# Thirty-two-row score products in attention, and batches taken in pairs through the layers before it

## The reference

```python
x = x + L0_xattn(_layernorm(x), ctx_1024)        # local attention-free mixing, then LN, 128->512->128 MLP, LN
x = x + L0_ffn(_layernorm(x))                    # gated FFN with 8-bit-like rounding of rows and ternary weights
x = x + L1_xattn(_layernorm(x), ctx, ctx, mask)  # 16 heads of 8 dimensions, 256 keys, softmax
x = x + L1_ffn(_layernorm(x))                    # top-1 routing to one of 8 experts, 128->256->128, gelu
```

## Time and profile before

| quantity | us |
|---|---|
| median of three runs | 248.2 |
| profiled execution | 249.16 |
| its span | 247.3 |
| PE busy | 192.6 (78%) |
| DVE busy | 173.2 (70%) |
| ACT busy | 135.4 (55%) |
| POOL busy | 119.1 (48%) |
| mean granted TensorE clock | 0.952 |

### The profile page before, as it was taken

The page is one execution under the profiler, slowest core; times in us unless marked ns, Lnnn a source line. Parts: engine busy times, 40 slices in busy tenths (PEclk is TensorE's granted clock), DMA queues, the critical chain, the costliest instruction groups (busy, mean ns, idle before and its releaser), DMA issues.

```text
span 247.3 us, 4771 instructions
## 1 busy us (share of the span) xinstructions
PE 192.6 (78%) x1750; PEld 134.4 (54%) x1750; DVE 173.2 (70%) x454; ACT 135.4 (55%) x271; POOL 119.1 (48%) x231
## 2 busy tenths in 40 slices
PE   0479865998328479776989988988897895999994
PEld 0358653897203177552433543543555784798883
DVE  4678888994684979869767786886755655739252
ACT  2246744939476578435767567667794256260100
POOL 8131768996649857831587784784221022000000
PEclk9999999999955789998899999999999997999999
DMA  5895040000000000000000000000000000000000
GB/s 169 324 398 219 0 170 4 0 4 0 3 1 0 0 0 3 3 3 3 0 0 5 1 0 3 0 3 0 3 1 3 0 0 4 0 3 21 24 21 21
DMA packets 4461, 8.75 MB, mean 35 GB/s; under 512 B 514, under 2 KB 3026, under 8 KB 4052
## 3 DMA queue, kind: packets, MB, share of 16 engines
q1 hardware_dynamic: 3636, 7.78, 8.4%
q10 hardware_dynamic: 800, 0.63, 0.8%
HBM read 7.89 MB, written 0.52 MB: 34 GB/s over the span
## 4 chain that ended last, share of the span: by engine, by line
PE 31%; POOL 29%; DVE 19%; issue 9%; ACT 7%; DMA 2%; SPq 1%; POOLq 0%; DVEq 0%
PE ps L1252 28%; POOL gate_pt L514 6%; POOL rstd L380 5%; POOL w L400 3%; PE ps L1261 3%; POOL x_in L431 3%; DMA wf<-weights_dram 2%; POOL w L392 2%; POOL vareps L377 2%; DVE gate_pt L1033 2%; DVE mx L1090 2%; DVE amax L1027 2%; DVE stats L798 2%; DVE half_c L1080 2%; ACT gate_pt L758 1%
## 5 line engine op out<-in xcount | busy, mean ns | idle before, releaser
L1090 DVE TENSOR_REDUCE mx<-ps 128x2 f32<-128x512 f32 x64 | 42.2, 686 | 16.6 <-PE ps L1252 16.5
L758 ACT ACTIVATE gate_pt<-ps 128x512 f32<-128x512 f32 x64 | 37.2, 603 | 15.6 <-PE ps L1252 15.3
L1252 PE MATMUL ps<-w,hid_xm 128*128 128x256 f16 (+1 forms) x288 | 30.3, 263 | 0.1
L514 POOL TENSOR_SCALAR gate_pt<-ka_mem 32x256 f16<-32x256 f16 x64 | 25.5, 399 | 4.4
L1252 PE MATMUL ps<-gate_pt,half_c 128*128 128x512 f16 x64 | 25.0, 393 | 3.2 <-issue 1.9
L1252 PEld LDWEIGHTS ps<-w,hid_xm 128*128 128x128 f16 x288 | 25.4, 101 | 3.4 <-issue 0.4
L1252 PE MATMUL ps<-qb,gate_pt 128*128 128x256 f16 x128 | 25.4, 281 | 0.8
L1261 PE MATMUL ps<-cst,rows 128*128 128x128 f32 x32 | 7.5, 333 | 18.0 <-ACT rows L662 8.8
L1252 PE MATMUL ps<-gate_pt,hid_xm 128*32 128x256 f32 x256 | 20.4, 390 | 1.5 <-ACT gate_pt L758 1.5
L1252 PEld LDWEIGHTS ps<-qb,gate_pt 128*128 128x128 f16 x128 | 9.5, 99 | 18.7 <-issue 11.4
L380 POOL TENSOR_TENSOR rstd<-vareps,halfs 128x2 f32<-128x2 f32 x24 | 17.7, 738 | 2.0
(11 more groups left out here) (221 smaller groups left out, 505.6 us busy)
## 6 DMA issues: line engine op xcount, KB each, us to landing
stage<-weights_dram SPq DMA_DIRECT2D x2, 1024.0 KB, 11.1
wf<-weights_dram SPq DMA_DIRECT2D x4, 256.0 KB, 8.5
wf<-mask_dram SPq DMA_DIRECT2D x1, 1024.0 KB, 4.8
eb_oT<-ffw_dram SPq DMA_DIRECT2D x1, 768.0 KB, 8.2
ctx_in<-ctx_rows_dram ACTq DMA_DIRECT2D x4, 128.0 KB, 5.9
x_in<-x_dram SPq DMA_DIRECT2D x4, 128.0 KB, 3.1
gate_pt<-ctx_cols_dram SPq DMA_DIRECT2D x1, 512.0 KB, 8.5
out_dram<-ctx_in SPq DMA_DIRECT2D x4, 128.0 KB, 1.7
```

The costliest lines, as they stand in the source:

```text
L514: ins = nc.gpsimd.tensor_scalar(kz[part, n % KRING, k], ka[part, b, quad], 1.0, 0.0, ALU.mult, ALU.add)
L758: nc_act(pt[:, head % PRING].rearrange("p t n -> p (t n)"), ps[:, 2 + head % 2, :], ACT.Exp, scale=DK ** -0.5).then_inc(sig["probs"], 1)
L1090: V.tensor_reduce(mx[:, b, head:head + 2, t], score_bank(4 * n + i).rearrange("p (h n) -> p h n", h=2), AX.X, ALU.max).then_inc(sig["smax" ...
L1252: return nc.tensor.matmul(dst, lhsT, rhs, start=start, stop=stop, skip_group_check=True)
```

## The change

Four edits come together.

1. Attention. The ring `kz`, its zeroing and `separated_keys` are gone. Score products take the 32 rows of one head directly from `ka`, `qa` and `qb`. A step issues four 256-column products (shifted tile 0, plain tile 0, shifted tile 1, plain tile 1); shifted head k lies in row strip k and the plain head in strip PLAIN_HEADS[k]. `weighted_values` goes from steps 0 and 1 of a quad to steps 0 and 2.
2. Routing of a batch on DVE is cut in three parts, at places 12, 13 and 14 of a tail; before it was one piece at place 13.
3. Pairs. Roots of LN_A (batches 2 and 3), LN_OUT and LN_FFN are taken for two batches in one instruction; the mean times root of LN_FFN goes to DVE; quantisation scales are computed for two batches at a time; the quantised rows, products and gate tiles of batches 0 and 1 are put ahead of the norms of batches 2 and 3.
4. Order. On PE the first and second MLP products of the batches are interleaved. On POOL the `beta` addition is gone (it is one DVE instruction over 128x1024 values now, ahead of DVE's split of `y`, together with the split of the key biases), the gated products come ahead of weight splits, and the splits of `wq` and `wo1` come later. On ACT the weight copies and the context copy move.

```diff
-KRING = 4
+PLAIN_HEADS = (2, 3, 0, 1)
-TAIL_STEPS = (0, 2, 4, 6, 10, 13, 15)
+TAIL_STEPS = (0, 2, 4, 6, 10, 12, 15)
+ROUTE_AT = (12, 13, 14)
...
-            def rstd_of(ln, b):
+            def rstd_of(ln, *bs):
+                cols = slice(bs[0], bs[-1] + 1)
+                pool.wait_ge(sig["ln_moments"], nth_norm(ln, bs[-1]))
...
+                nc.gpsimd.tensor_tensor(rstd[:, ln, cols, :].rearrange("p b t -> p (b t)"),
+                                        vareps[:, ln, cols, :].rearrange("p b t -> p (b t)"),
+                                        halfs[:, 0:len(bs) * TILES], ALU.pow).then_inc(sig["ln_rstd"], 1)
...
+            gated(0)
+            gated(1)
             a, z = SEG["wo"]
             pool.wait_ge(sig["w_hi"], 2)
...
+            gated(2)
+            gated(3)
             split_lo("w1", 3)
+            rstd_of(LN_A, 0)
+            rstd_of(LN_A, 1)
+            rstd_of(LN_A, 2, 3)
             split_lo("w2", 4)
...
-            for b in range(B):
-                for t in range(TILES):
-                    ins = nc.gpsimd.tensor_tensor(xb[:, b, t], x_in[:, b, t], beta_b[:, :], ALU.add)
...
             for first in range(0, B, 2):
-                for b in (first, first + 1):
-                    rstd_of(LN_OUT, b)
-                for b in (first, first + 1):
-                    rstd_of(LN_FFN, b)
-                    rows_shift(LN_FFN, b)
+                rstd_of(LN_OUT, first, first + 1)
+                rstd_of(LN_FFN, first, first + 1)
...
-            def separated_keys(n):
...
-                for k in range(4):
-                    part = slice(32 * k, 32 * k + 32)
-                    ins = nc.gpsimd.tensor_scalar(kz[part, n % KRING, k], ka[part, b, quad], 1.0, 0.0, ALU.mult, ALU.add)
...
+            ffn_rows(0)
+            ffn_rows(1)
...
+            round_rows(0)
+            round_rows(1)
+            key_hi(0, 0)
+            key_hi(1, 0)
+            quantised_columns(0)
+            quantised_columns(1)
+            gate(0)
+            gate(1)
+            ffn_rows(2)
+            ffn_rows(3)
...
+            V.tensor_tensor(xb[:, :, :, :].rearrange("p b t n -> p (b t) n"), x_in[:, :, :, :].rearrange("p b t n -> p (b t) n"),
+                            beta_b[:, :].unsqueeze(1).to_broadcast([P, B * TILES, D]), ALU.add).then_inc(sig["xb"], 1)
+            dve.wait_ge(sig["mbias_hi"], 1)
+            V.scalar_tensor_tensor(kb16[0:2, :], kb_h[:, :], c("lo_2", 2), kb_in[:, :], ALU.mult, ALU.add)\
+                .then_inc(sig["mbias_ready"], 1)
...
+            def scores_tile(n, i, t, masked):
+                b, quad = divmod(n, QUADS)
+                head = rows_of(PLAIN_HEADS[i])
+                dst = score_bank(i)[:, t * T:(t + 1) * T]
+                ins = mm(dst, qa[head, b, quad, t * P:(t + 1) * P], ka[head, b, quad], True, not masked)
...
+            def shifted_tile(n, k, t, masked):
+                b, quad = divmod(n, QUADS)
+                tok = slice(t * P, (t + 1) * P)
+                dst = ps[:, 2 + k % 2, t * T:(t + 1) * T]
+                ins = mm(dst, ka[rows_of(k), b, quad, tok], qb[rows_of(k), n % 2], True, not masked)
...
+            def shifted_beside_plain(n, k, masked):
+                shifted_wait(n, k)
+                plain = n + 2 < B * QUADS
+                if plain:
+                    scores_wait(n + 2, k)
+                for t in range(TILES):
+                    shifted_tile(n, k, t, masked)
+                    if plain:
+                        scores_tile(n + 2, k, t, masked)
...
-                        if k < TILES and n >= 1:
-                            weighted_values(n - 1, k)
+                        if k % 2 == 0 and n >= 1:
+                            weighted_values(n - 1, k // 2)
```

More of the change, by code:

```diff
@@ L90, in nth_norm, with nth_root, nth_shift, nth_max @@
     return nth(ln, b)
+ROOTS = [(LN_IN, (0,)), (LN_IN, (1,)), (LN_IN, (2,)), (LN_IN, (3,)), (LN_A, (0,)), (LN_A, (1,)), (LN_A, (2, 3)),
+         (LN_OUT, (0, 1)), (LN_FFN, (0, 1)), (LN_OUT, (2, 3)), (LN_FFN, (2, 3)),
+         (LN_ATT, (0,)), (LN_ATT, (1,)), (LN_ATT, (2,)), (LN_ATT, (3,)),
+         (LN_MOE, (0,)), (LN_MOE, (1,)), (LN_MOE, (2,)), (LN_MOE, (3,))]
+def nth_root(ln, b):
+    return 1 + [b in bs and of == ln for of, bs in ROOTS].index(True)
+def nth_shift(ln, b):
+    return b // 2 + 1 if ln == LN_FFN else B // 2 + b + 1
+MAXIMA = ["row 0", "row 1", "gate 0", "row 2", "gate 1", "row 3", "gate 2", "gate 3", "gate 4", "gate 5", "gate 6", "gate 7"]
+def nth_max(kind, n):
+    return MAXIMA.index(f"{kind} {n}") + 1
+def nth_scale(b, row):
+    return B // 2 + b + 1 if row else b // 2 + 1
 def nth_of_tail(stage, b, moe):
@@ L1137, in tail_dve @@
                     ins.then_inc(sig["top8"], 1)
+                if part == 1:
                     dve.wait_ge(sig["top8"], b + 1)
@@ L1220, in _ @@
             tail_dve(3, 0)
-            tail_dve(2, 5)
+            for part in range(3):
+                route(2, part)
             tail_dve(3, 1)
@@ L1231, in _ @@
             tail_dve(3, 4)
-            tail_dve(3, 5)
+            for part in range(3):
+                route(3, part)
             gelu_lo(1)
```

429 lines of the change are left out of this document (245 added, 184 removed).

## The result

| | before | after |
|---|---|---|
| median of the comparison runs | 248.34 us (247.9 to 249.67) | 261.24 us (257.12 to 264.54) |
| profiled execution, its span | 249.16, 247.3 | 257.12, 255.3 |
| mean granted TensorE clock | 0.952 | 0.858 |
| POOL busy | 119.1 us | 81.6 us |

The ratio of after to before is 1.0389, 95% interval 1.0321 to 1.0456. The forecast was 239.0 us, range 230 to 248: wrong in sign, and outside the range. This ratio and every other one here compares the faster executions only (of after 257.12 and 258.89 us; the other two took 263.59 and 264.54 at a clock down to 0.823), so it isn't the quotient of the medians, which are of all executions. What follows on after reads the profiled one, the fastest.

A forecast was written before the change was run, and what follows sets the result against it. Bound by POOL early, DVE in the gate stage, PE's order in attention. 249.16 - 4.6 (early layers) - 4.4 (attention) = 240.2 us; less 0.96 us for the profiled execution's excess over the median, 239.2, say 239; range 230 to 248.

The forecast's parts named there:

- The clock in attention: Attention: granted TensorE clock expected to stay at 1.00, with nothing for it in the sum.
- the rival: Attention: clock falls, each us at 1.2 GHz costing about half; 30 us of it give 254 us; chance 0.05.
- The strips: Attention score products: two row strips overlap, step 0.30 us instead of 0.45, saving 0.6 us a quad on PE before switches.
- The rival that strips don't overlap: Attention: strips run one after another with weight loads bare, step 0.55 us, total 256 us; chance 0.06.
- POOL's copies vanish: 0, since they ran beside it: Attention: dropping POOL's key copies gains 0 us.
- Order in attention: Attention: moved weighted values and split routing together gain 0.2 us in a tail quad, bounds 0 to 0.5.
- Values at 0 and 2: Attention: weighted values at steps 0 and 2 keep ACT and DVE supplied; part of 0.2 us a tail quad.
- Routing in parts: Attention tails: DVE's 1.2 us routing piece becomes three, counted as part of a 0.2 us gain in a tail quad.
- The early layers: Before attention: first gate product at 69.2 instead of 77.19 us, gate stage ends at 84.9 instead of 89.5, minus 4.6 us.
- PE work is unchanged, I carry this as 1 us: LN_A and interleaved MLP: delay carried as 1 us, last ff_mm at 58.6 us instead of 57.6.
- Beta: Early layers: addition leaves POOL (minus 6.44 us there), costs DVE 1.2 us; with the key bias, 1.1 us delay at wo.
- minus 4.4: Attention's whole term: 6 quads at 0.35 us and 9 at 0.25 us saved; bounds minus 11 and plus 13.

The follow-up runs named there:

- Experiments 9 and 12: Before with after's PE order in attention, and after whole, both with score products on all 128 rows: 249.07 us, ratio 1.0032, and 252.61 us, ratio 1.0153.
- 4: After with PLAIN_HEADS = (0, 1, 2, 3), so that a step's plain and shifted products share one row strip: 285.56 us, ratio 1.1516.
- experiment 5: Before with the paired 32-row step and weighted values at steps 0 and 2 in quads 6 to 15 only: 256.18 us, ratio 1.0285.
- experiment 7: Before with only the weighted values moved, to steps 0 and 2 of each quad: 247.35 us, ratio 0.9955.
- experiment 11: After's early layers with beta on POOL and routing in three parts, before's full-height scores, weighted values at steps 0 and 2: 251.59 us, ratio 1.0007 to before.

## Why the prediction failed, by its own steps

**The clock in attention: the step that decided.** The prediction took every quad at 1.00, because it stood there before with PE 88% busy. This term was put at nothing in the sum. It named the rival and gave it 0.05, although it also said that the profile can't tell. Measured, the light quads ran wholly at 0.50 and the stretch from 137.6 to 180 us at 0.78. With 30 us at half clock it gave 254 us; the windows of after make 0.68 over the 65.8 us, which is 42 us at half clock. Its price of half a us for each us at 1.2 GHz was too high: a light quad took 4.93 us at 0.50, 1.2 us more than before's at 1.00 and 1.5 more than the 3.4 forecast, which is 0.25 and 0.31 us for each us at half clock. Experiments 9 and 12 show the cause, 4 that busy time is no guide.

**The strips: right on PE, and of no use.** Pairs within 10 ns, step 0.24 against the forecast 0.30. The rival that strips don't overlap is refuted. At the full clock they shortened quad 7 from 4.91 to 4.65 us and quad 8, with the copies still there, not at all (5.34, experiment 5).

**"POOL's copies vanish: 0, since they ran beside it": wrong, and not for the result.** The root of LN_MOE waited 1.2 us behind them in the quads with a norm; where they are gone, quad 8 took 4.32 us for 5.34.

**Order in attention.** Values at 0 and 2: right in sign, and about 1 us in all (experiment 7), where the prediction had not separated it from the strips. Routing in parts: wrong in sign, plus 1.6 us in the quads of two profiles (experiment 11) where a gain was counted.

**The early layers.** Moments of batch 1 at LN_OUT were put at 56 us and came at 58.94. That is the mis-sized term: "PE work is unchanged, I carry this as 1 us" left out the mask's transfer, DVE's new order and a first-layer product now ahead of batch 1's second layer. From the moments to the first gate product the sum was right: 13.2 us forecast, 58.94 to 71.95 = 13.0 measured. The gate stage then took 16.4 us, 15.7 forecast; two small scale instructions of the second pair took 0.95 and 0.97 us, 0.17 and 0.14 for the first pair, while POOL combined the masks (four instructions from 75.49 us on). The end at 88.3 us is 0.9 ahead of before (89.20 in its trace, where the prediction has 89.5), and PE's products of LN_ATT at 100 to 104 us, 0.84 us a group of three at half clock instead of 0.49, gave that back and more: first score at 107.40 for 106.86.

**Beta.** Its own price was right (1.21 us for 1.2), the key bias cost 1.21 for 0.94, the delay at LN_A's statistics was 38.23 - 36.43 = 1.8 us for 1.1. POOL's slower `y` beside it was not in the sum. With beta on POOL the layers went from 1.016 to 1.0028. The relief of POOL, the 2.81 us of DVE's wait for the root, did come: 0.46 us were left; but the work ahead had become late instead.

**The sum of after** is then: plus 1.1 us to the first query copy where minus 4.6 stood, plus 7.6 in attention where minus 4.4 stood, minus 0.8 behind it where 0 stood. That gives 257.1 us, the profiled execution.

## What to carry to other kernels

A product that uses fewer rows of the array saves time at a given clock and may lose the clock, and then every full-size product near it takes longer too, here 1.02 us for 0.57 and 0.64 for 0.38. Before narrowing products in a stretch where PE sets the pace, run the same order once with narrow operands and once with full-height ones, and read the granted clock by quads, not the busy share. When work leaves an engine that seems to have time to spare, look at what stands behind it in that engine's list: the copies on POOL held up a root that PE waited for. And when an instruction is moved, follow its buffer: here the split of one weight matrix set the start of a transfer 11.7 us on, on which a third engine's order hung.
